# Turning expert tokens once, and copying them to the second 64 partitions on VectorE

## What is computed

```python
x = x + _L0_conv_ref(_ln_c(x), ...)
t = _to_tokens(x)
t = t + _L0_ffn_ref(_ln_t(t), ...)
# _L0_ffn_ref:
gate_logits = xf @ Wg + bg
top_w, top_i = jax.lax.top_k(gate_logits, 2)
top_w = jax.nn.softmax(top_w, axis=-1)
for e in range(E):
    h = jax.nn.gelu(xf @ W1[e] + b1[e], approximate=False)
    out = out + w_dense[:, e:e + 1] * (h @ W2[e] + b2[e])
```

## Time and profile before

| | us |
|---|---|
| median of 3 runs | 2283.13 |
| lowest and highest | 2280.98, 2287.26 |
| profiled execution, its time | 2289.27 |
| profiled execution, its span | 2287.5 |
| PE busy | 1959.1 |
| DVE busy | 1456.3 |
| POOL busy | 972.4 |

### The profile page before, as it was taken

The page is one execution under the profiler, slowest core; times in us unless marked ns, Lnnn a source line. Parts: engine busy times, 40 slices in busy tenths (PEclk is TensorE's granted clock), DMA queues, the critical chain, the costliest instruction groups (busy, mean ns, idle before and its releaser), DMA issues. The chain is left out here.

```text
span 2287.5 us, 34748 instructions
## 1 busy us (share of the span) xinstructions
PE 1959.1 (86%) x11630; PEld 1105.3 (48%) x11630; DVE 1456.3 (64%) x2524; ACT 785.5 (34%) x1382; POOL 972.4 (43%) x1038
## 2 busy tenths in 40 slices
PE   8985898787989999999999984408999999999955
PEld 5652444344555545555555544304555555555534
DVE  4444566565878977989779886624555555555534
ACT  4431111111223223232232322305556666666620
POOL 8001000100224351443514537764777777777740
PEclk9987999898999999999999995559999999999976
DMA  9767888887888787887888733236666666566439
GB/s 289 165 135 184 203 199 208 205 193 200 210 204 218 212 208 206 229 217 206 215 209 223 217 98 112 64 87 158 165 157 168 169 161 163 156 169 167 109 114 357
DMA packets 265829, 419.09 MB, mean 183 GB/s; under 512 B 116224, under 2 KB 188452, under 8 KB 242685
## 3 DMA queue, kind: packets, MB, share of 16 engines
q1 hardware_dynamic: 160701, 348.14, 57.6%
q0 software_dynamic: 32352, 39.58, 6.6%
q10 hardware_dynamic: 72608, 29.25, 5.4%
HBM read 337.34 MB, written 89.60 MB: 187 GB/s over the span
## 5 line engine op out<-in xcount | busy, mean ns | idle before, releaser
L951 POOL DMA_INDIRECT token_rows<-gate_rows,gate_index x392 | 414.5, 1057 | 662.2 <-DVE gate_index L1280 548.5
L1158 DVE TENSOR_TENSOR prod<-z_ps,r_all 119x896 f32<-119x896 f32 x512 | 542.7, 1083 | 126.3 <-PE z_ps L1071 100.9
L1473 POOL DMA_INDIRECT mixed<-exp_mix,exp_xt x474 | 479.8, 1012 | 193.2 <-issue 154.2
L1075 PE MATMUL z_ps<-xq,band 112*119 112x448 f32 x1024 | 438.1, 563 | 70.5 <-DVE prod L1158 70.4
L1491 ACT ACTIVATE exp_hid<-exp_h_ps,exp_pack 128x384 f32<-128x384 f32 x632 | 329.7, 574 | 263.0 <-PE exp_h_ps L1529 263.0
L1075 PEld LDWEIGHTS z_ps<-xq,band 112*119 112x119 f32 x1024 | 181.5, 186 | 277.0 <-issue 174.2
L1529 PE MATMUL exp_h_ps<-exp_tok,exp_pack 64*128 64x384 f32 x1264 | 247.5, 510 | 0.0
L984 ACT ACTIVATE ob<-o_ps 128x448 f32<-128x448 f32 x64 | 34.8, 544 | 601.8 <-PE o_ps L1088 601.8
L1088 PE MATMUL o_ps<-prod,pick 119*32 119x448 f32 x2048 | 238.6, 559 | 1.2 <-DVE prod L1158 0.3
L1537 PE MATMUL exp_y_ps<-exp_hid,exp_pack 128*64 128x384 f32 x1264 | 230.9, 486 | 0.0
L1571 DVE COPY exp_tok<-exp_x_ps 128x384 f32<-128x384 f32 x158 | 88.1, 557 | 223.6 <-PE exp_x_ps L1516 219.5
(11 more groups left out here) (195 smaller groups left out, 2051.8 us busy)
## 6 DMA issues: line engine op xcount, KB each, us to landing
xq<-xs SPq DMA_DIRECT2D x192, 896.0 KB
exp_pack<-packs SPq DMA_DIRECT2D x158, 258.5 KB
exp_xt<-token_rows SPq DMA_DIRECT2D x158, 120.0 KB
xs<-xpad SPq DMA_DIRECT2D x32, 448.0 KB, 5.9
co<-ob ACTq DMA_DIRECT2D x64, 224.0 KB, 16.2
xin<-in_x_dram SPq DMA_DIRECT2D x8, 1568.0 KB, 11.9
merge_yt<-mixed ACTq DMA_DIRECT2D x28, 448.0 KB, 6.4
mixed<-exp_mix,exp_xt POOLq DMA_INDIRECT x474
```

The lines of the kernel that those rows point to most:

```text
L951: pool.indirect_dma_start(out=token_rows[:, :], out_offset=bass.IndirectOffsetOnAxis(ap=index[b % RR][:, j:j + 1], axis=0), in_=rows[b % R ...
L1075: mm = nc.tensor.matmul(zt, band[t % BR][rows_in, at:at + MF], maps, start=True, stop=True)
L1158: nc.vector.tensor_tensor(prod[(NU * t + u) % PR][:, :, :].rearrange("p m (d x) -> p m d x", d=D), z_ps[(NU * t + u) % 3][0:MF, :, 0:CN].r ...
L1473: pool.indirect_dma_start(out=mixed[:, :], out_offset=bass.IndirectOffsetOnAxis(ap=xt[t % XT][:, j, ROW_ID:ROW_ID + 1].bitcast(U32), axis= ...
```

## The change

For each block of 128 tokens there is now one transpose in place of two matmuls with the identity, and it writes partitions 0 to 63 of `x_ps` alone. DVE copies these 64 partitions to the first half of `tok`, which raises `tok_done`; it waits for that, and copies the first half of `tok` to partitions 64 to 127, SBUF to SBUF, which raises the new semaphore `tok_again`. `turn` still waits for `tok_done`; `hidden` waits for `tok_again`.

```diff
                 for j in range(TILE_BLOCKS):
-                    for e in range(2):
-                        mm = nc.tensor.matmul(x_ps[C * e:C * (e + 1), P * j:P * (j + 1)],
-                                              xt[t % XT][:, j, 0:C], ident[:, :], start=True, stop=True)
+                    mm = nc.tensor.transpose(x_ps[0:C, P * j:P * (j + 1)], xt[t % XT][:, j, 0:C], ident[:, :])
                 mm.then_inc(turned, 1)
...
                 if hb == 0:
-                    pe.wait_ge(tok_done, t + 1)
+                    pe.wait_ge(tok_again, t + 1)
...
                 if t >= 3:
                     dve.wait_ge(h_done, (t - 2) * 4)
-                nc.vector.tensor_copy(tok[t % 3][:, :], x_ps[:, 0:N]).then_inc(tok_done, 1)
+                nc.vector.tensor_copy(tok[t % 3][0:C, :], x_ps[0:C, 0:N]).then_inc(tok_done, 1)
+                dve.wait_ge(tok_done, t + 1)
+                nc.vector.tensor_copy(tok[t % 3][C:P, :], tok[t % 3][0:C, :]).then_inc(tok_again, 1)
```

More of the change, by code:

```diff
@@ L1412, in expert_stage @@
         tok_done = sem("tok_done")
+        tok_again = sem("tok_again")
         h_done = sem("h_done")
```

## The result

| | before | changed |
|---|---|---|
| median of 8 runs each, us | 2285.99 | 2267.07 |
| lowest and highest, us | 2280.98, 2289.16 | 2261.34, 2275.98 |
| profiled execution, its time, us | 2289.27 | 2268.61 |
| its span, us | 2287.5 | 2266.7 |

The ratio of the changed kernel to the one before is 0.9925, with a 95% interval of 0.9908 to 0.9942: 17 us faster, between 13 and 21. The forecast was 8.7 us faster, with a range down to 2263. The direction and the bound behind it hold; the size is twice what was forecast.

The account below looks back on a forecast made before the run. PE bounds the expert stage, with POOL 16.8 us behind. -16.8 (waits) + 3.5 + 5 (copy) + 3 (adds) - 3.4 (`add_conv`) = -8.7 us, taking the median from 2283.13 to 2274.4; range 2263 to 2292.

Parts of the forecast that it names:

- the bound behind it: Expert stage: PE bounds it before, POOL 16.8 us behind; after the change POOL becomes the bound and these waits go.
- random phases: DVE operations start anywhere in POOL's 1.29 us scatter cycle: hold-ups of 3.5 + 5 (copy), 3.5 (adds), 10.0 us (`add_conv`).
- the pace alone: PE's `turn`: three transposes without change-over cost, 0.33 us as lower bound; upper bound 0.48, taken 0.38.

Follow-up runs that it names:

- half_out_before: The kernel before with the second block of `outputs` (two of four matmuls of the second expert layer) left out; 0.9919 of before.
- half_out_after: The changed kernel with two of the four matmuls of the second expert layer left out; 0.9973 of the kernel before.

## What to carry to other kernels

Before counting what an edit takes off the bounding engine, work out the bare pace of the next one from a stretch where it is behind: busy share (75% here) hid that POOL was within 5% of full. Where a DVE operation on SBUF runs beside GpSimd's indirect DMAs, ask what lies over the start of each DMA; the length of the operation there, and what it pushes later, count for more than its number. If two engines have the same pace, phases can persist, and an average over random phases then says little about either outcome.

## What was not expected of the hardware

- A scatter (0.98 us) is held up only over its start: it ends 0.86 us after the end of a DVE operation that covers it, whether that has two SBUF inputs or is a copy of SBUF to SBUF (0.85 to 0.87 us in 146 cases in six profiles). A copy that begins 0.04 us or less ahead of the scatter waits itself, and a copy from PSUM does neither.
- The same copy, begun between 0.5 and 0.8 us into a scatter, waits itself until about 0.81 and takes up to 0.63 us in place of 0.35; begun at 0.1 to 0.5 it neither waits nor holds anything up.
- PE lost part of what three transposes in place of six matmuls should save: `outputs` is 0.05 us longer behind the three transposes (1.44 against 1.39), and `turn` takes 0.45 where the pace alone would make it 0.33 (the prediction's estimate). That this is the price of a change between transposes and float32 matmuls is likely; no run isolates it.
- In half_out_before and half_out_after PE's granted clock fell to 0.50 for 3 to 7 us at a time in the middle of the stage, after idle gaps of 1.9 to 3.8 us; other gaps as long had no fall behind them.
